# Last stage of a two-layer adaptive mixture-of-experts and int8 feed-forward kernel: int8 activations transposed as pairs of bytes, PSUM copies on two engines, second matrix two tiles behind

## The reference

```python
def act_quant(x):
    scale = 127.0 / jnp.clip(jnp.max(jnp.abs(x), axis=-1, keepdims=True), 1e-05)
    q = jnp.clip(jnp.round(x * scale), -128.0, 127.0) / scale
...
def bitlinear(x, w, b):
    xq = act_quant(rmsnorm(x))
    wq = weight_quant(w)
    return jnp.einsum('bsd,fd->bsf', xq, wq) + b
h = bitlinear(x, w1, b1)
h = jax.nn.gelu(h, approximate=False)
return bitlinear(h, w2, b2)
```

## Time and profile before

| | |
|---|---|
| median of 3 runs | 885.37 us (883.66 to 886.49) |
| the profiled execution's own time | 881.29 us |
| its span, first to last instruction | 879.5 us |
| mean granted clock of TensorE, share of full | 0.942 |
| TensorE matmul busy | 768.5 us (87%) |
| VectorE busy | 532.7 us (61%) |
| ScalarE busy | 490.1 us (56%) |
| GpSimd busy | 339.6 us (39%) |

### The profile page before, as it was taken

How to read it: one execution, slowest core, us unless ns; L and a number is a source line. 1 busy time by engine, 2 the same in 40 slices (tenths; PEclk the granted TensorE clock), 3 DMA queues, 4 the chain that set the end, 5 groups by cost and what they waited for, 6 DMA issues and landing times. The chain is left out here.

```text
span 879.5 us, 10973 instructions
## 1 busy us (share of the span) xinstructions
PE 768.5 (87%) x3828; PEld 495.0 (56%) x3828; DVE 532.7 (61%) x1029; ACT 490.1 (56%) x682; POOL 339.6 (39%) x330
## 2 busy tenths in 40 slices
PE   5774799998999999634999999975799999999997
PEld 3321277776777777412777777764355555555553
DVE  2672445454455455214465565543799999999995
ACT  1110226664377778414566556632687777777783
POOL 0486413243142122204444444420254555444553
PEclk9987789999999999856999999987899999999999
DMA  6999427897295486331111102000012221222212
GB/s 203 347 414 334 146 107 273 288 318 239 97 257 130 131 229 145 43 131 48 49 49 49 40 19 88 1 1 10 27 49 72 73 69 64 68 65 73 72 62 82
DMA packets 42534, 109.07 MB, mean 124 GB/s; under 512 B 4208, under 2 KB 4992, under 8 KB 39280
## 3 DMA queue, kind: packets, MB, share of 16 engines
q1 hardware_dynamic: 35616, 94.71, 30.4%
q0 software_dynamic: 6352, 13.06, 8.0%
q10 hardware_dynamic: 512, 0.61, 0.2%
HBM read 88.63 MB, written 28.13 MB: 133 GB/s over the span
## 5 line engine op out<-in xcount | busy, mean ns | idle before, releaser
L1297 PE MATMUL ps<-ff_q,qt 128*128 128x512 bf16 x512 | 123.8, 387 | 7.1 <-DVE h L1362 6.3
L1323 PE MATMUL ps<-ff_q,ht 128*128 128x512 bf16 x512 | 115.7, 379 | 2.4 <-DVE ht L1379 2.4
L824 PE MATMUL ps<-w_h,inner_l 128*128 128x512 f32 x256 | 102.8, 401 | 3.6 <-DVE inner_l L773 3.6
L1283 POOL TENSOR_SCALAR hb<-h 128x2048 bf16<-128x2048 int8 x32 | 60.8, 1900 | 111.2 <-ACT h L1341 111.2
L639 POOL DMA_INDIRECT x_after_experts<-y,row_of_slot x32 | 51.4, 1605 | 134.7 <-DVE y L759 127.4
L826 PE MATMUL ps<-w_h,inner_h 128*128 128x512 f32 x256 | 101.2, 395 | 0.0
L825 PE MATMUL ps<-w_l,inner_h 128*128 128x512 f32 x256 | 101.1, 395 | 0.0
L1341 ACT ACTIVATE h<-h,to_q 128x2048 int8<-128x2048 f32 x32 | 64.1, 2002 | 44.3 <-DVE to_q L1393 44.3
L1362 DVE SCALAR_TENSOR_TENSOR h<-ps,scale,bias 128x1024 f32<-128x1024 f32 x64 | 81.6, 1279 | 9.3 <-PE ps L1297 9.3
L773 DVE SCALAR_TENSOR_TENSOR inner_l<-ps,inner_h 128x512 fp32r<-128x512 f32 x64 | 44.2, 691 | 69.9 <-ACT inner_h L708 69.4
L1297 PEld LDWEIGHTS ps<-ff_q,qt 128*128 128x128 bf16 x512 | 49.4, 99 | 64.0 <-DVE h L1362 7.5
(11 more groups left out here) (211 smaller groups left out, 1516.1 us busy)
## 6 DMA issues: line engine op xcount, KB each, us to landing
w_in_sb<-in_w_in_t SPq DMA_DIRECT2D x8, 2048.0 KB, 12.7
w_raw<-in_w_out_t SPq DMA_DIRECT2D x16, 1024.0 KB, 5.5
raw<-in_ff_t SPq DMA_DIRECT2D x16, 1024.0 KB, 7.6
xt<-in_x_t SPq DMA_DIRECT2D x8, 1024.0 KB, 9.3
x_after_experts<-in_x SPq DMA_DIRECT2D x8, 1024.0 KB, 16.8
x_sum<-x_after_experts SPq DMA_DIRECT2D x8, 1024.0 KB, 4.8
x<-x_after_experts SPq DMA_DIRECT2D x32, 256.0 KB, 2.7
out<-res SPq DMA_DIRECT2D x32, 256.0 KB, 2.0
```

What stands on the lines that cost most here:

```text
L824: pe.matmul(ps[:, s, :], inner_l[:, k % 2, c], w_h[:, k % RING, :], start=k == 0, stop=False)
L1297: m = pe.matmul(ps[:, f, :], qt[:, t, k, :], ff1_q[:, k, f * 512:(f + 1) * 512], start=k == 0, stop=k == KD - 1)
L1323: m = pe.matmul(ps[:, OUT[t3 % 2], :], ht[:, k, :], ff2_q[:, k, :], start=k == 0, stop=k == KF - 1)
```

## The change

**Transposes.** The int8 tile h8 is no longer cast. Two int8 values that lie side by side are taken as one 16-bit value, so that 8 transposes of 128 x 128 move the whole tile, into one PSUM bank; tiles alternate between the two banks. A transposed 16-bit value holds two neighbours of h in its two bytes. The copies out of PSUM view the bank as int8, take one byte of each pair with a stride of two bytes, and write bf16 (the view `pair_v`): `ht` is ordered by pair, byte, token. So that the second matrix meets the same order, `raw_view` loads two neighbouring rows of ff2 for each partition.

**Copies.** ScalarE does the first half (4 of 8 pair blocks), VectorE the second, and waits for ScalarE's.

**Lag.** Transposes, copies and second matrix of tile i - 2 (before i - 3) stand in turn i, and the result of tile i - 3 (before i - 4). The result, the sum with x, moves on VectorE from the end of the turn to the place between the joined maximum and the four small operations. SyncE issues the load of x1 ahead of the store.

```diff
-                return ff2_t[g * GK * P:(g + 1) * GK * P, :].rearrange("(k p) f -> p k f", p=P)
+                return ff2_t[g * GK * P:(g + 1) * GK * P, :].rearrange("(m p a) f -> p m a f", p=P, a=2)
...
+            LAG2 = 2
+            pair_v = [ps[:, TRH[i], :].bitcast(I8).rearrange("p (m c a) -> p m a c", m=KF // 2, a=2) for i in (0, 1)]
...
-                            pool.wait_ge(h8_ready, t + 1)
-                            if t >= 2:
-                                pool.wait_ge(h_tr, 2 * (t - 1))
-                            pool.tensor_scalar(hb[:, t % 2, :], h8[:, t % 2, :], 1.0, 0.0, ALU.mult, ALU.add).then_inc(hb_ready, 1)
...
+                            pe.wait_ge(h8_ready, t2 + 1)
+                            if t2 >= 2:
+                                for c in h_cp:
+                                    pe.wait_ge(c, t2 - 1)
+                            pairs = h8[:, t2 % 2, :].bitcast(BF16)
+                            bank = ps[:, TRH[t2 % 2], :].bitcast(BF16)
+                            for m in range(KF // 2):
+                                tr = pe.transpose(bank[:, m * P:(m + 1) * P], pairs[:, m * P:(m + 1) * P], ident_b[:])
+                            tr.then_inc(h_tr, 1)
...
-                                    pe.wait_ge(h_cp, 2 * t3 + 1 + k // (KF // 2))
+                                    pe.wait_ge(h_cp[2 * k // KF], t2 + 1)
...
-                    for i in range(TILES + 1):
-                        t0, t1 = i, i - 1
+                    for i in range(TILES + LAG2):
+                        t0, t1, t2 = i, i - 1, i - LAG2
+                        if inside(t2, TILES):
+                            act.wait_ge(h_tr, t2 + 1)
+                            if t2 >= 1:
+                                act.wait_ge(f2, t2)
+                            act.activation(ht[:, 0:KF // 4, :, :], pair_v[t2 % 2][:, 0:KF // 4, :, :], ACT.Copy).then_inc(h_cp[0], 1)
...
-                                act.wait_ge(hb_ready, t1 - 1)
+                                act.wait_ge(h_tr, t1 - 1)
...
-                        if inside(t3, TILES):
-                            if t3 >= 1:
-                                ve.wait_ge(f2, t3)
-                            for half in (0, 1):
-                                ve.wait_ge(h_tr, 2 * t3 + half + 1)
-                                ve.tensor_copy(ht[:, half * (KF // 2):(half + 1) * (KF // 2), :].rearrange("p k c -> p (k c)"),
-                                               ps[:, TRH[half], :].bitcast(BF16)).then_inc(h_cp, 1)
+                        if inside(t2, TILES):
+                            ve.wait_ge(h_cp[0], t2 + 1)
+                            ve.tensor_copy(ht[:, KF // 4:, :, :], pair_v[t2 % 2][:, KF // 4:, :, :]).then_inc(h_cp[1], 1)
```

More of the change, by code:

```diff
@@ L1244, in build @@
             small2, to_q2 = sem("small2"), sem("to_q2_ready")
-            h8_ready, hb_ready, h_tr, h_cp = sem("h8_ready"), sem("hb_ready"), sem("h_tr"), sem("h_cp")
+            h8_ready, h_tr, h_cp = sem("h8_ready"), sem("h_tr"), [sem(f"h_cp_{i}") for i in ("act", "ve")]
             f2, done, xb_ready, half2 = sem("f2"), sem("done"), sem("xb_ready"), sem("half2_ready")
@@ L1255, in _ @@
                     sp.dma_start(bias2[:], ff2_b.partition_broadcast(P)).then_inc(bias2_in, DMA)
[L1256 to L1259, removed]
+                    for i in range(TILES + LAG2 + 1):
                         if inside(t := i, TILES):
@@ L1263, in _ @@
                             sp.dma_start(x1[:, t % 2, :], x1_v2[t]).then_inc(x1_in[t % 2], DMA)
+                        if inside(t := i - LAG2 - 1, TILES):
+                            sp.wait_ge(done, t + 1)
+                            sp.dma_start(out_v[t], res[:, t % 2, :]).then_inc(stored[t % 2], DMA)
                     for p in (0, 1):
@@ L1299, in first_matrix @@
                         m.then_inc(f1, 1)
-                    for i in range(TILES + 3):
-                        t0, t3 = i, i - 3
+                    for i in range(TILES + LAG2):
+                        t0, t2 = i, i - LAG2
                         if inside(t0, TILES):
                             first_matrix(t0, 0)
-                        if inside(t3, TILES):
-                            pe.wait_ge(hb_ready, t3 + 1)
-                            for half in (0, 1):
-                                if t3 >= 1:
[L1309 to L1314, removed]
+                        if inside(t2, TILES):
[8 more added lines that the diff above has]
+                            tr.then_inc(h_tr, 1)
@@ L1315, in _ @@
                         if inside(t0, TILES):
                             first_matrix(t0, 1)
-                        if inside(t3, TILES):
-                            if t3 >= 2:
-                                pe.wait_ge(done, t3 - 1)
+                        if inside(t2, TILES):
+                            if t2 >= 2:
+                                pe.wait_ge(done, t2 - 1)
                             for k in range(KF):
                                 if k % (KF // 2) == 0:
-                                    pe.wait_ge(h_cp, 2 * t3 + 1 + k // (KF // 2))
-                                m = pe.matmul(ps[:, OUT[t3 % 2], :], ht[:, k, :], ff2_q[:, k, :], start=k == 0, stop=k == KF - 1)
+                                    pe.wait_ge(h_cp[2 * k // KF], t2 + 1)
+                                m = pe.matmul(ps[:, OUT[t2 % 2], :], ht[:, k // 2, k % 2, :], ff2_q[:, k, :], start=k == 0, stop=k == KF - 1)
@@ L1368, in half_max @@
                                          apply_absolute_value=True).then_inc(h_max, 1)
-                    for i in range(TILES + 4):
-                        t0, t1, t3, t4 = i, i - 1, i - 3, i - 4
+                    for i in range(TILES + LAG2 + 1):
+                        t0, t1, t2, t3 = i, i - 1, i - LAG2, i - LAG2 - 1
                         if inside(t0, TILES):
                             add_bias(t0, 0)
-                        if inside(t3, TILES):
-                            if t3 >= 1:
-                                ve.wait_ge(f2, t3)
-                            for half in (0, 1):
-                                ve.wait_ge(h_tr, 2 * t3 + half + 1)
-                                ve.tensor_copy(ht[:, half * (KF // 2):(half + 1) * (KF // 2), :].rearrange("p k c -> p (k c)"),
-                                               ps[:, TRH[half], :].bitcast(BF16)).then_inc(h_cp, 1)
+                        if inside(t2, TILES):
+                            ve.wait_ge(h_cp[0], t2 + 1)
+                            ve.tensor_copy(ht[:, KF // 4:, :, :], pair_v[t2 % 2][:, KF // 4:, :, :]).then_inc(h_cp[1], 1)
                         if inside(t1, TILES):
@@ L1385, in _ @@
                             s(ve.tensor_tensor(big, mx[:, t1 % 2, 0:1], mx[:, t1 % 2, 1:2], ALU.max))
+                        if inside(t3, TILES):
+                            ve.wait_ge(f2, t3 + 1)
+                            ve.wait_ge(xb_ready, t3 + 1)
+                            if t3 >= 2:
+                                ve.wait_ge(stored[t3 % 2], DMA * (t3 // 2))
+                            ve.scalar_tensor_tensor(res[:, t3 % 2, :], ps[:, OUT[t3 % 2], :], scale2[:, t3:t3 + 1],
+                                                    xb[:, t3 % 2, :], ALU.mult, ALU.add).then_inc(done, 1)
+                        if inside(t1, TILES):
                             ve.wait_ge(rms2_ready, t1 + 1)
@@ L1396, in _ @@
                             add_bias(t0, 1)
[L1397 to L1403, removed]
 def kernel(**inputs):
```

3 lines of the change are left out of this document (1 added, 2 removed).

## The result

| | before | after |
|---|---|---|
| median | 884.51 us (4 runs, 883.03 to 886.49) | 962.97 us (4 runs, 962.26 to 963.73) |
| span of the profiled execution | 879.5 us | 960.5 us |
| its own time | 881.29 us | 962.31 us |

The changed kernel is slower by a factor of 1.0886, 95% interval 1.0859 to 1.0912. The forecast was 972 us, with a range of 948 to 985.

The account below looks back on a forecast made before the run. TensorE was taken to bound the kernel at 7.80 us a tile. Thirty turns of 10.62 us less 0.74, with 0.6 more tail, added 86.4 us: 967.7 profiled, 972 us for the median, range 948 to 985.

Parts of the forecast that it names:

- The loop: Through VectorE's and ScalarE's queues, ADD1 to the next tile's ADD1: new waits close a loop of 10.62 us against 7.80.
- VectorE's copy to the maximum: On VectorE, from the start of its int8 copy out of PSUM to the second half's maximum: 1.20 us.
- ScalarE's copy and hand-over: From the start of ScalarE's copy to that of VectorE's: 1.05 us of copy and 0.05 of hand-over, 1.10 us.
- the result: On VectorE, the moved sum with x, ahead of the small operations: delays to_q by its 0.74 us.
- The tail: From the last tile's ADD1 to the end: 20.2 us against 19.6, or +0.6.
- the two ends for VectorE's copy: VectorE's int8 copy from PSUM: 0.60 us below (bf16 copy), 1.20 above (f32 read); 1.20 taken, quick copy chance 0.10.
- ADD1: On VectorE, the bias add into the second half of h; predicted to repeat every 10.6 us.
- the bank of the first matrix's second half: On TensorE, a wait of about 0.9 us a tile for this bank, before the wait for ScalarE's copy.
- The parts costed at nothing: SyncE's load of x1 ahead of the store, at nothing; ff2 rows in pairs, within 0.2 us either way.
- The clock: Rival: TensorE's new gaps lower its clock; a mean down to 0.69 is free, at 0.66 the time is 987; chance 0.06.
- ADD0: On VectorE, the bias add into the first half of h; 1.20 us.
- Work alone decides: Rival at the wait ahead of VectorE's copy: the loop doesn't close; 879 us, or 871 with the quick copy; chance 0.04.

Follow-up runs that it names:

- the wait: Changed kernel with VectorE's copy waiting for TensorE's transposes, not ScalarE's copy, and the transposed halves in two PSUM banks: 909.92 us, 1.0288.
- the square's place: Changed kernel with the square behind ScalarE's copy in ScalarE's queue instead of ahead of it, all waits unchanged: 900.87 us, 1.0186.
- the turn without the result: Changed kernel with the result moved back to the end of VectorE's turn, behind the second bias add: 944.28 us, 1.0676.
- the one with the quick copy: Changed kernel with VectorE's copy reading 1024 16-bit integers without a stride instead of bytes at a stride of two: 947.53 us, 1.0728.
- the lag of three: Changed kernel with transposes, copies and second matrix three tiles behind, and the result four: 965.53 us, 1.0922.
- The last kernel: Kernel of "copy ahead of ADD0" with the joined maximum taking one tensor and a scalar instead of two tensors: 876.27 us, 0.9902.
- copy ahead of ADD0: Kernel of "halves swapped" with VectorE's result and copy placed ahead of the first bias add: 902.47 us, 1.0219.
- one engine: Changed kernel with VectorE copying the whole transposed tile in one 2048-byte instruction, ScalarE's copy taken out: 921.97 us, 1.0432.
- GpSimd's sum moved: Kernel of "copy ahead of ADD0" with GpSimd's sum of x and bias ahead of the mean square: 903.32 us, 1.0227.
- halves swapped: Changed kernel with VectorE copying the first half after TensorE's transposes, ScalarE the second, waiting for VectorE: 887.38 us, 1.0044.

## Why the prediction was right

*The loop* held. Every step of it is in the rows, in that order, and both its cuts (the wait, the square's place) gave what its sum said within 7 us of some 60 (53 us for 60, 62 for 59); the turn without the result and the one with the quick copy met 9.73 and 9.86 within 0.02.

*Its size* was 10.62, measured 10.40. Three terms were a little long: VectorE's copy to the maximum, 1.20 taken and 1.14 measured (I took the distance of an operation with an f32 PSUM input); ScalarE's copy and hand-over, 1.10 and 1.04 (its own 1.00 us, 1.05 taken); the result, 0.74 and 0.67. Over 30 turns this is 6 us. The tail was 20.2 us, as predicted (940.34 to 960.5), the start 0.55 us later. Together the span grew by 81.0 us where the sum said 86.4. The other 3.5 us between 972 and 963 come from the profiled execution of before, which lay further under its median than that of after.

*The copies.* Of the two ends for VectorE's copy the upper was right; the runs add that the stride has no part in it.

*The gaps.* VectorE's 2.88 us (2.9 said), TensorE's 2.06 for ScalarE's copy (2.3 said), ScalarE's 3.14 for to_q and 0.32 for ADD1 (3.0 and 0.3 said). One was named wrongly: TensorE's other wait, 0.66 us, isn't for the bank of the first matrix's second half but ahead of the transposes, for the int8 step (L1344). It lies off the loop, and the lag of three showed that it is worth nothing; the wait for the bank is behind it and came out there, at 0.49 us where 0.9 was said.

*The parts costed at nothing.* SyncE's new order and the ff2 rows in pairs were in every experiment, and none took them out alone. The last kernel has them too, at 876 us.

*The clock* did fall now and then, as that rival said, and cost nothing, as its threshold said. From 640 to 680 the granted clock is 0.91, above, so part of it at 1.2 GHz; the second matrix of one tile took 5.30 us and not 3.6 (TensorE's timeline), VectorE's next ADD0 came 0.84 us late, and ADD1 still came after 10.41 us, 10.40 and 10.41 (VectorE's timeline):

```profile
654.02 5.30 PE L1321 MATMUL ps<-ff_q,ht 128*128 128x512 bf16 x15 [2.06 <-ACT ht L1337]
```

```profile
648.56 2.47 DVE L1365 SCALAR_TENSOR_TENSOR h<-ps,scale,bias 128x1024 f32<-128x1024 f32 x2
658.97 1.27 DVE L1365 SCALAR_TENSOR_TENSOR h<-ps,scale,bias 128x1024 f32<-128x1024 f32 x1
661.09 1.28 DVE L1365 SCALAR_TENSOR_TENSOR h<-ps,scale,bias 128x1024 f32<-128x1024 f32 x1 [0.84 <-PE ps L1295]
669.38 2.47 DVE L1365 SCALAR_TENSOR_TENSOR h<-ps,scale,bias 128x1024 f32<-128x1024 f32 x2
679.79 1.28 DVE L1365 SCALAR_TENSOR_TENSOR h<-ps,scale,bias 128x1024 f32<-128x1024 f32 x1
```

From 710 to 830 us the granted clock stayed at 1.00, with the same gap of 2.06 us in every tile, so the gap alone doesn't decide it; what does, no run here shows. The Trainium skill ("TensorE: Matmul & The Clock Gate", "A second HAM failure mode: psum-queue depth-cycling") says that the clock swings when TensorE idles briefly between groups of matmuls, and that this costs throughput. The trace agrees in part: the clock swings in some stretches and not in others, and it had no price, since TensorE isn't what sets the pace.

*Work alone decides*: the rival of the other side was wrong for the change as written, but the last kernel comes out between its two sums. It has the change's transposes and split copies, another order and another form of the joined maximum, and takes 876 us where the rival said 871 and 879.

What was expected of the experiments failed three times by more than 7 us: by 28 (copy ahead of ADD0) and 16 (one engine), where the step left out was that a VectorE operation can be held by GpSimd, and by 29 (GpSimd's sum moved), where it was GpSimd's own ring. The hold had no place in the prediction, since before and after the change the sum of x and bias falls beside other operations.

## What to carry to other kernels

Before splitting a step over two engines, walk from each new wait backwards through the queue that must answer it and forwards through the queue that waits, and add up the loop; here every engine had room and the loop was 10.4 us. If two engines must take turns at a buffer, let the one whose queue comes to it first go first, and give the consumer that half first: here this brought back 76 of 78 us, where taking VectorE's wait for ScalarE out had brought back 53. An instruction that takes several times its usual duration, with no wait shown, is to be laid beside what the other engines do at that moment.

## What the runs showed of the hardware

- VectorE reads int8 from PSUM at about half the pace of 16-bit values: 1.225 against 0.69 us for 1024 elements (1.14 against 0.61 from start to start), with a stride of two bytes or none. From SBUF the int8 cast of 2048 elements took 1.227 us, from PSUM 2.28 (one engine).
- A VectorE operation with two tensors in SBUF that comes up while GpSimd adds two tensors in SBUF is held until GpSimd's ends: 1.15 us and not 0.16 for one column, 28 times of 28 (640 to 880 us, copy ahead of ADD0). In the kernel with one engine it took from 0.23 to 0.74 us from 640 us on, as it met the sum later or earlier, and always ended with it. It isn't held if it starts first (0.16 us, halves swapped), nor with a scalar pointer in place of the second tensor (0.21 us), nor with its first tensor in PSUM (the result, 0.75 us, halves swapped). No run shows it beside another operation on GpSimd. The Trainium skill, "GPSIMD Engine Reference", section "8. Key points", says that GpSimd shares its SBUF interfaces with VectorE, in contention with instructions of two SBUF inputs; the trace agrees.
- The change's wait of VectorE for ScalarE has a reason in the Trainium skill, "PSUM — Partial Sum Buffer", section "PSUM bank collisions raise a hardware error": no two engines may access one bank in the same partitions at once, readers included. No run here shows it: either the copies were ordered or they had a bank each.
